# Moving the layer norms' combining of statistics from VectorE, tile by tile, to GpSimd, all tiles at once

## What is computed

```python
h = tok(x)                                        # frames @ DCT basis
h = h + attn(layernorm(h))
h = h + ffn(layernorm(h))

def attn(x):                                      # 4 heads
    n = layernorm(x, ln1_g, ln1_b)
    ...                                           # shift mix, q k v g, rmsnorm, decayed linear-attention scan
    x = x + (g * att) @ Wo.T
    return x + gelu(layernorm(x, ln2_g, ln2_b) @ W1.T) @ W2.T

def ffn(x):
    a = layernorm(x, ln_g, ln_b) @ attn_w.T + attn_b + x
    ...                                           # gelu(a @ fc1) @ fc2, gelu(. @ next_w)
```

## Time and profile before

| | us |
|---|---|
| median of 3 runs | 1221.79 |
| lowest, highest | 1215.12, 1226.37 |
| the profiled execution | 1218.9 |
| its span (first to last instruction) | 1217.1 |
| PE busy | 1138.9 (94%) |
| DVE busy | 986.5 (81%) |
| ACT busy | 621.5 (51%) |
| POOL busy | 300.9 (25%) |

### The profile page before, as it was taken

One profiled execution on the slowest core, in us unless ns is written; L12 is line 12 of the kernel. 1 busy time (PEld: TensorE's weight loads), 2 busy tenths in 40 slices (PEclk: granted clock), 3 DMA queues, 4 the chain that ended last, 5 costly groups with the idle time before them and its releaser, 6 DMA issues.

```text
span 1217.1 us, 43497 instructions
## 1 busy us (share of the span) xinstructions
PE 1138.9 (94%) x17955; PEld 807.8 (66%) x17955; DVE 986.5 (81%) x3362; ACT 621.5 (51%) x1100; POOL 300.9 (25%) x174
## 2 busy tenths in 40 slices
PE   4799999999999999999999999999999999999997
PEld 4576676666767676766666667666676766667664
DVE  7878788797887979788796887979879797987962
ACT  3346446363554736446363554736446364554634
POOL 4123131221403223131311403223131221403211
PEclk8799999999999999999999999999999999999999
DMA  5321313222141312313222141312313222141210
GB/s 188 106 64 39 113 43 110 65 79 56 43 132 44 87 47 66 110 43 113 63 78 55 44 130 46 88 45 63 112 44 110 63 80 57 43 132 45 87 55 17
DMA packets 51492, 91.48 MB, mean 75 GB/s; under 512 B 9536, under 2 KB 26592, under 8 KB 51296
## 3 DMA queue, kind: packets, MB, share of 16 engines
q1 hardware_dynamic: 51296, 88.69, 24.1%
HBM read 19.50 MB, written 9.78 MB: 24 GB/s over the span
## 4 chain that ended last, share of the span: by engine, by line
PE 83%; DVE 9%; POOL 4%; issue 3%; ACT 2%; DVEq 0%; POOLq 0%
PE bank L1056 10%; PE bank L1049 9%; PE bank L1084 9%; PE bank L1078 8%; PE bank L919 8%; PE bank L914 7%; PE bank L1014 7%; PE bank L998 5%; PE bank L990 4%; PE bank L1033 4%; POOL nrm L391 3%; PE bank L1029 3%; PE bank L954 3%; PE bank L943 2%; PE bank L994 2%
## 5 line engine op out<-in xcount | busy, mean ns | idle before, releaser
L514 ACT ACTIVATE px<-bank 128x512 f32<-128x512 f32 (+1 forms) x128 | 72.8, 569 | 218.0 <-PE bank L998 152.9
L763 DVE COPY_PREDICATED px<-mask,bank 128x512 f32<-128x512 uint32 (+1 forms) x128 | 88.6, 692 | 79.6 <-issue 76.8
L1078 PE MATMUL bank<-xa,f1w 128*128 128x512 f32 (+1 forms) x256 | 124.7, 587 | 14.8 <-DVE qtok L704 13.0
L1056 PE MATMUL bank<-w,hid 128*128 128x128 f32 x1024 | 121.9, 277 | 17.2 <-ACT hid L533 17.2
L1056 PEld LDWEIGHTS bank<-w,hid 128*128 128x128 f32 x1024 | 116.7, 192 | 31.6 <-ACT hid L533 31.6
L1014 PEld LDWEIGHTS bank<-qx,ki 128*32 128x32 f32 x7680 | 89.6, 110 | 42.3 <-issue 33.9
L827 DVE TENSOR_TENSOR ki<-k,rp 128x96 f32<-128x96 f32 (+13 forms) x512 | 113.2, 295 | 0.6 <-ACT k L499 0.6
L397 POOL TENSOR_TENSOR ab<-af,heads 128x896 f32<-128x896 f32 x16 | 40.8, 2552 | 291.1 <-DVE af L755 291.1
L1049 PE MATMUL bank<-c,w 128*128 128x512 f32 (+1 forms) x256 | 111.4, 568 | 1.1 <-ACT c L527 0.9
L1084 PE MATMUL bank<-hid,f2w 128*128 128x512 f32 (+1 forms) x256 | 107.5, 563 | 0.0
L1014 PE MATMUL bank<-qx,ki 128*32 128x16 f32 x7680 | 99.2, 193 | 6.9 <-issue 6.6
(11 more groups left out here) (142 smaller groups left out, 2414.0 us busy)
## 6 DMA issues: line engine op xcount, KB each, us to landing
qx<-qq SPq DMA_DIRECT2D x256, 96.0 KB
hs<-hs SPq DMA_DIRECT2D x32, 532.0 KB, 4.4
v<-v_f SPq DMA_DIRECT2D x16, 512.0 KB, 3.9
gz<-gate_f SPq DMA_DIRECT2D x16, 512.0 KB, 4.7
xT<-in_xT SPq DMA_DIRECT2D x16, 468.5 KB, 4.0
f1w<-in_fc1T SPq DMA_DIRECT2D x16, 256.0 KB, 2.7
f2w<-g_dram SPq DMA_DIRECT2D x16, 256.0 KB, 3.0
out<-t_sum SPq DMA_DIRECT2D x16, 256.0 KB, 2.7
```

Source lines behind the costliest of these rows:

```text
L763: V.copy_predicated(px[c % 2][0:n, :, 0:n], mask[0:n, 0:n].rearrange("p (o m) -> p o m", o=1).to_broadcast([n, HEADS, n]), bank[DIAG][0:n, ...
L1056: last = mm(dst[:, P * i:P * i + P], hid[:, j, P * m:P * m + P], w2[:, j, :], start=(j == 0), stop=(j == 3))
L1078: mm(dst[:, 0:width[g]], f1w[:, P * j:P * j + P], xa[:, cols(g)], start=True, stop=True).then_inc(f1_ok, 1)
```

## The change

The three pairs of DVE steps `gathered` and `vv` go. In their place GpSimd, ahead of each power, combines the even and odd numbers itself, for all tiles of the set at once: sum of the means and of the squared deviations, difference of the means, its square times 32, the sum of these, half the sum of means as the mean, and `vv` from the sum. Each instruction that reads what GpSimd has just written waits on GpSimd's own semaphore first. The order of the other work is kept, but GpSimd's first wait is now for `bn_stats` and not for `vv`.

```diff
+            def moments(st, mv, sums, odd, s, up, n):
+
+                gp.tensor_tensor(sums[:, s, :], st[:, s, 1:3], st[:, s, 4:6], ALU.add)
+                gp.tensor_tensor(odd[:, s], st[:, s, 1], st[:, s, 4], ALU.subtract).then_inc(up, 1)
+                gp.wait_ge(up, n + 1)
+                gp.tensor_tensor(odd[:, s], odd[:, s], odd[:, s], ALU.mult)
+                gp.tensor_scalar(mv[:, s, 0], sums[:, s, 0], 0.5, None, ALU.mult).then_inc(up, 1)
+                gp.wait_ge(up, n + 2)
+                gp.tensor_scalar(odd[:, s], odd[:, s], 32.0, None, ALU.mult).then_inc(up, 1)
+                gp.wait_ge(up, n + 3)
+                gp.tensor_tensor(odd[:, s], odd[:, s], sums[:, s, 1], ALU.add).then_inc(up, 1)
+                gp.wait_ge(up, n + 4)
+
+            def twice_normed(vv, odd, s, up, n):
+
+                gp.tensor_scalar(vv[:, s, 0], odd[:, s], 1.0 / P, EPS, ALU.mult, ALU.add)
+                gp.tensor_scalar(vv[:, s, 1], odd[:, s], (1.0 + EPS) / P, EPS * EPS, ALU.mult, ALU.add).then_inc(up, 1)
+                gp.wait_ge(up, n)
...
             def pow3(b, g):
-                gp.wait_ge(var3, nth(b, 2, g + 1))
+                gp.wait_ge(bn3, nth(b, 2, g + 1))
+                before(gp, n2_ok, b, 2, g + 1)
+                moments(st3, mv3, sm3, od3, four(g), mo3, nth(b, 10, 5 * g))
+                twice_normed(vv3, od3, four(g), mo3, nth(b, 10, 5 * g + 5))
...
-            def gathered(mv, st, ms, ag, count):
-                V.memset(tick[:, :], 0.0)
-                for m in ms:
-                    last = V.bn_aggr(mv[:, m, :], st[:, m, :])
-                last.then_inc(ag, 1)
-                dve.wait_ge(ag, count)
...
             def stats3(b, g):
                 dve.wait_ge(h1_ok, nth(b, 2, g + 1))
+                before(dve, r3_ok, b, 2, g + 1)
                 stats(h1, st3, bn3, g)
-                dve.wait_ge(bn3, nth(b, 2, g + 1))
-                gathered(mv3, st3, tiles(g), ag3, nth(b, 2, g + 1))
-                twice_normed(vv3, mv3, four(g)).then_inc(var3, 1)
```

More of the change, by code:

```diff
@@ L112, in program @@
         st1, vv1 = sb("st1", TILES, 6), sb("vv1", TILES, 2)
+        (sm1, od1), (sm2, od2), (sm3, od3) = ((sb(f"sm{i}", TILES, 2), sb(f"od{i}", TILES)) for i in (1, 2, 3))
         hl = sb("hl", PADT + 1)
@@ L169, in program @@
         ge2 = sem("ge2"); fin_ok = sem("fin_ok")
[L171 removed]
+        bn1 = sem("bn1"); mo1, mo2, mo3 = sem("mo1"), sem("mo2"), sem("mo3"); nl_ok = sem("nl_ok"); d_ok = sem("d_ok")
         mix = [sem(f"mix{i}") for i in range(4)]
@@ L376, in _ @@
             gp.memset(zq[:, :], 1.0)
+            gp.memset(hs0[:, SH:], 0.0)
             for tile in (hl, mixed[0], mixed[1]):
@@ L382, in _ @@
             gp.wait_ge(s_init, 2)
-            def pow1(b):
-                gp.wait_ge(var1, nth(b, 1, 1))
+            def moments(st, mv, sums, odd, s, up, n):
[13 more added lines that the diff above has]
+                gp.wait_ge(up, n)
+            def pow1(b):
+                all_ = slice(0, TILES)
+                gp.wait_ge(bn1, nth(b, 2, 2))
+                before(gp, hs1_in, b, 16, 16)
+                moments(st1, mv1, sm1, od1, all_, mo1, nth(b, 5, 0))
+                twice_normed(vv1, od1, all_, mo1, nth(b, 5, 5))
                 gp.tensor_tensor(rr1[:, :, :], vv1[:, :, :], nhalf[:, :].rearrange("p (m o) -> p m o", o=2), ALU.pow).then_inc(r1_ok, 1)
@@ L401, in pow2 @@
             def pow2(b, g):
-                gp.wait_ge(var2, nth(b, 2, g + 1))
+                gp.wait_ge(bn2, nth(b, 2, g + 1))
+                before(gp, nl2_ok, b, 2, g + 1)
+                moments(st2, mv2, sm2, od2, four(g), mo2, nth(b, 10, 5 * g))
+                gp.tensor_scalar(vv2[:, four(g)], od2[:, four(g)], 1.0 / P, EPS, ALU.mult, ALU.add).then_inc(mo2, 1)
+                gp.wait_ge(mo2, nth(b, 10, 5 * g + 5))
                 gp.tensor_tensor(rr2[:, four(g)], vv2[:, four(g)], nhalf[:, 0:4], ALU.pow).then_inc(r2_ok, 1)
@@ L642, in stats @@
                 last.then_inc(bn, 1)
-            def gathered(mv, st, ms, ag, count):
-                V.memset(tick[:, :], 0.0)
-                for m in ms:
-                    last = V.bn_aggr(mv[:, m, :], st[:, m, :])
-                last.then_inc(ag, 1)
-                dve.wait_ge(ag, count)
-            def twice_normed(vv, mv, s):
-                V.tensor_scalar(vv[:, s, 0], mv[:, s, 1], EPS, None, ALU.add)
-                return V.tensor_scalar(vv[:, s, 1], mv[:, s, 1], 1.0 + EPS, EPS * EPS, ALU.mult, ALU.add)
             def stats1(b, g):
                 dve.wait_ge(h_cp, nth(b, 2, g + 1))
+                before(dve, r1_ok, b, 1, 1)
                 stats(h, st1, bn1, g)
[L660 to L664, removed]
             def normed(b):
@@ L778, in stats2 @@
                 dve.wait_ge(x2_ok, nth(b, 2, g + 1))
+                before(dve, r2_ok, b, 2, g + 1)
                 stats(x2, st2, bn2, g)
-                dve.wait_ge(bn2, nth(b, 2, g + 1))
-                gathered(mv2, st2, tiles(g), ag2, nth(b, 2, g + 1))
-                V.tensor_scalar(vv2[:, four(g)], mv2[:, four(g), 1], EPS, None, ALU.add).then_inc(var2, 1)
             def normed2(b, g):
@@ L841, in body @@
                 if (b := at(1)) is not None:
[L842 to L846, removed]
+                    gated(b, 1); attended(b, 1); stats2(b, 1)
                 if (b := at(0)) is not None:
```

4 lines of the change are left out of this document (2 added, 2 removed).

## The result

| us | before | changed kernel |
|---|---|---|
| median of the runs taken side by side | 1219.97 (4 runs) | 1274.73 (4 runs) |
| lowest, highest | 1215.12, 1226.37 | 1269.59, 1275.95 |
| span of the profiled execution | 1217.1 | 1274.0 |
| PE busy, idle within the span | 1138.9, 78.2 | 1154.7, 119.3 |

The ratio is 1.0438, with a 95% interval of 1.0379 to 1.0496: 4.4% slower, 55 us. The sign was forecast, the size was not: 18.7 us were forecast, and the top of the range, 1259, is exceeded.

The account below looks back on a forecast made before the run. PE was taken as the bound, 94% busy, waiting 0.87 us a round for DVE's `qtok`. 15 x 1.2 + 0.7 = 18.7 us on the profiled 1218.9 gave 1237.6, stated as 1238, range 1221 to 1259.

Parts of the forecast that it names:

- The durations of small instructions: New GpSimd instructions: 0.20 us each, 0.10 more for a second in a group, 0.08 per wait; sets of 1.70 or 1.60 us.
- pow1 and pow2(1): First norm's set and half 1 of the second's: normed2(1) ends at 601.7, PE wants it at 602.01; no cost.
- a sign of being wrong: Prediction called itself wrong if, among other signs, PE's transposes of nl2(1) waited for DVE.
- dear instructions: Rival: 0.40 us per small instruction, PE waits 2.2 us at the transposes, 4.2 a round, 1282 us; chance 0.12.
- the term that counts: Third norm, half 0: DVE's `d` and mix hold GpSimd, `nb` 1.2 us too late each round, PE's `qtok` wait 2.1 us.
- the weaker: PE needs ACT's L538 after `nb` of normed3(0) only at 611.68, so `nb` may end at 609.98, against 609.41 via `qtok`.
- I price it at nothing: Third norm, half 1: DVE slips 0.8 us, but PE uses the spread q only at 630.82; no cost.
- The start: Bare chain at the kernel's start: 1.70 us in place of some 0.9 for eight tiles, +0.7 us.
- Too cheap: Rival: small instructions at 0.10 us cost 0.4 us a round, 1225; not held by DVE at all, 1219; chance 0.32.
- faster: Rival: powq(0) starts earlier and PE's 0.87 us wait a round shrinks, at most 13 us, 1206; chance 0.04.
- the tiles of normed hold GpSimd: Rival: pow2(1)'s groups wait for DVE's L672 tiles, PE waits 0.3 to 1.0 us more, up to 1253; chance 0.08.

Follow-up runs that it names:

- s12: Kernel before with the first norm's set and both halves of the second norm's combined on GpSimd, the third norm's on DVE; 1236.03 us, ratio 1.0121.
- free: Kernel before with only the first norm's set and half 0 of the second norm's combined on GpSimd; 1219.63 us, ratio 1.0025.
- s3: Kernel before with only the third norm's sets, both halves, combined on GpSimd; 1251.76 us, ratio 1.0249.
- s31: Kernel before with only half 1 of the third norm's statistics combined on GpSimd; 1241.18 us, ratio 1.0182.
- s30: Kernel before with only half 0 of the third norm's statistics combined on GpSimd; 1246.73 us, ratio 1.0220.
- afterlate: Changed kernel, all five sets on GpSimd, with normed3(1) moved behind the q levels on DVE; 1253.97 us, ratio to the kernel before 1.0306.
- x31late: s31 with normed3(1) moved behind the q levels on DVE; 1222.29 us, ratio to the kernel before 1.0029.
- swapb: Kernel before, no set on GpSimd, with x_attn(0) moved ahead of mixes(2) on DVE; 1205.09 us, ratio 0.9863.

## Why the prediction was right and wrong

**The durations of small instructions: right for one, wrong for a step.** 0.20 us for one is what the rows of pow1 show (0.20 to 0.24). The first pair starts 0.17 us apart, but from then on each instruction of pow1 starts 0.27 to 0.33 us after the one before, whether it waits for it or not: the second and third pair, taken as 0.10 more for their second instruction, cost a whole 0.27 more (622.74 to 623.01, 623.94 to 624.21). 2.22 us and 2.17 stand where 1.70 and 1.60 were forecast.

**pow1 and pow2(1), "no cost, but only 0.3 us of cover": the step that failed first.** The two sets are 1.09 us longer than forecast together, a cover of 0.3 was left, and PE waits 0.8 us a round at the transposes of nl2(1), which the prediction had named as a sign of being wrong. The working was right in its frame (the rival "dear instructions" named this very place, deciding "from 0.22 us an instruction on"), but I weighed the rival by the instruction's own duration, when what decides is the pitch, from start to start: 15 x 0.8 = 12 us of waits, +15.8 in all (s12). free shows that nothing is lost until pow2(1)'s set comes behind pow1's.

**pow3(0), "the term that counts": the mechanism right, the limit wrong.** Held by `d` and the mix as told: 4.0 us from first instruction to power (3.5 forecast), `nb` beside resid(1) 1.22 us, 2.69 us idle before it (2.4 forecast). But PE's wait at `qtok` did not grow from 0.87 to 2 us, it stayed 0.87. PE stops earlier, at the transposes behind ACT's L570, which I had called "the weaker" limit; and since the products of q's second half stand behind those, the loop from the transposes over ACT's squares, DVE's sums and powq back to PE is only shifted: from the transposes of `x` to the products it is 649.49 - 642.67 = 6.82 us, 6.68 before. The cost is 0.75 us a round at this place, 0.44 of it (6.6 us in s3) from pow3(0) and the rest with the first two norms' lateness. 10.5 us by s3 less s31, where 18 were forecast; alone it costs 27.1 (s30), where the 0.55 us that the forecast counts on are not there. One reading in the working is off: resid(1) ended 607.99 - 606.86 = 1.13 us after the mix's end, not 1.28; nothing in the sum rests on it.

**pow3(1), "I price it at nothing": wrong, and the largest.** Forecast 0.8 us of slip, "were no slack there, 0.8 us a round". It slipped 1.17 us, since this chain too is longer than forecast (2.14 us in place of 1.70), and its lateness cost 21.0 us alone and 18 to 21 in the changed kernel (afterlate), 1.2 to 1.4 us a round. I had looked for the first product that reads the spread q, saw 7 us up to it in a timeline of one round and took them for slack. But the q levels and the transfer lie in between. The records of the DMA packets show how much was left (us; half 0 of q is four DMAs of 32 packets):

```
kernel   first packet  last packet  PE's first product  PE's wait before it
before   626.98        629.47       630.82              0
x31late  628.49        630.99       632.33              0
changed  659.27        661.77       662.15              0.14
changed  279.69        283.39       283.92              1.48
```

In the kernel before PE begins 1.1 to 1.4 us after the last packet in every round but the first (0.75). In the changed kernel and in s31 it begins 0.38 to 0.59 us after it in nearly every round (0.74 once; in both the first round stands apart), and waits there. So of the 1.35 us some 0.96 were cover (an estimate: 1.35 less the shortest 0.39 or so). By it the forecast's own slip of 0.8 would have stayed inside, and 1.17 did not. What was late is the input of these products, and the profile names no engine for it.

**Where those 21 us are.** In s31 PE's idle time and busy time grew by 12.4 and 8.3 us. The idle part is the issue waits. From the restart of PE at L1078's place to the first product on the spread q it is 12.46 us in the mean before and 12.88 in s31, which is the late q: 0.4 us a round, 6 in all. From there to the next restart it is 60.49 and 61.37: 0.9 a round, 13 in all, lost behind the late q. In most rounds of the changed kernel the wait for q is short, as at 662.15. Its three longest (1.38, 1.48 and 0.97 us; the 1.48 is that at 283.92) fall where the spread's packets took 3.1 to 3.7 us in place of 2.5, with a piece of PE's code beside them.

These pieces bear on the rest as well. They come over the queue named instruction, 144 of 16 KB in the kernel before, the changed one and s31 alike, while DVE's and GpSimd's instructions change in number. ACT's 1100 are too few for 2.36 MB; for PE's 17955 products and as many weight loads it is 66 bytes each, so I take them for PE's code. In the profile of the changed kernel every stall of 0.35 us or more inside a run of L997 or L1021 ends 1.3 to 1.6 us after such a piece has arrived, as the records of that queue show (us):

```
kernel   piece starts, takes   arrives   stall ends, length
changed  663.14  1.55          664.69    666.06  0.75
changed  669.92  1.38          671.30    672.69  1.53
changed  740.09  1.75          741.84    743.30  0.94
changed  818.80  1.47          820.27    821.71  0.66
before   133.89  0.93          134.82    136.33  0.91
before   280.15  1.70          281.85    283.16  1.14
```

Of all 23 issue waits of the kernel before, 22 end 1.2 to 1.7 us after a piece arrived, of the changed kernel's 40 it is 32 (27.8 of 29.9 us), while such stretches cover only 7% of the span; the 8 others all stand before the first product on the spread q. Pieces took 0.9 to 1.5 us with no other packet beside them and up to 1.9 with many. A piece starts when PE has come to a point: for three in four of the 144, PE had by then begun the same number of instructions as before, to within 20. Products on the spread q are among the shortest of all (0.20 us each), so the code is used up fastest there; at 663.14 a piece starts one microsecond after PE began them, while the spread of q's other packets is still under way. That this is why more is lost behind the late q than the q is late by is what the records suggest; no run changed the fetch itself, so it stays argued. That the order on DVE decides it is shown (x31late).

**The busy time.** The granted clock is part of it. In the stretch from 700 to 800 us of the changed kernel (us, PE, PEld, DVE, ACT, POOL busy, PEclk, DMA share, GB/s)

```profile
700.00:800.00 100.00, 92.16 (x1244) 66.67 (x1243) 71.59 (x209) 48.37 (x87) 40.22 (x72) 0.97 0.22 67
```

and in that of the kernel before

```profile
700.00:800.00 100.00, 95.55 (x1759) 66.40 (x1758) 83.32 (x280) 54.47 (x99) 20.71 (x11) 1.00 0.30 88
```

the clock is 0.97 in place of 1.00: it stood at half (1.2 in place of 2.4 GHz) for 6.8 us from 745 us on, after the stall that ended at 743. After 75 us the clock was at half for 17.1 us in the changed kernel, in four pieces, 13.7 in s31, 3.4 in s12 and none in before. At half speed 17.1 us lose at most 8.6, of the 15.8 by which PE's busy time grew. x31late had 10.2 us of it and lost next to nothing, so the clock isn't what tells s31 from x31late. The remaining 7 us or more of busy time are not settled.

**The sum as it came out.** Priced places, in us: first and second norm 15.8 (forecast 0, or 0.7 with the start), third norm half 0 10.5 (18.0), half 1 21.0 (0): 47.3, and 7.5 more when all five sets are together. The start was forecast at +0.7 and came to 1.8 by the waits for `nl` of normed (4.6 us, 2.8 before). The two terms that the forecast set at nothing are 36.8 us, two thirds of the loss. The share of the third norm's halves hangs on which is counted first (27.1 and 4.4 by s30), but putting half 1's lateness right in the changed kernel gave back 18 to 21 us. And the forecast was 1237.6 for an execution 2.9 us below the median, so 1240.5 and not 1238 for the median.

**The rivals.** "Too cheap" is out by the held 1.15 us; "faster" is out, as the argument had it for this change, though its mechanism, powq(0) earlier and PE's 13 us gone, is real and was had in swapb by another edit. "Dear instructions" was the nearest to the truth in place and had a chance of only 0.12. Of "the tiles of normed hold GpSimd" there is a little: two of the tensor_scalar ones in pow2(1), beside L687's tiles, take 0.34 and 0.36 us, those of pow1 0.20 to 0.24. The Trainium skill (SBUF — State Buffer, section "Who interferes with whom") has two-input DVE instructions and GpSimd's excluding each other for their whole length; by the 1.15 us under `d` and the 1.14 under the mix the trace agrees. The other way round it does not in the kernel before, where `d` started beside a power and took its usual 1.14 us.

## What to carry to other kernels

On an engine that hands on by semaphore price a chain of small instructions by its pitch from start to start, not by the duration of one: here 0.27 to 0.33 us for 0.20. This error of 0.4 to 0.6 us a set stands behind both terms that were set at nothing. Before work moves onto the chain of a less busy engine, compare the length added with the cover at each consumer in turn, the last one in the round too, and where a transfer lies in between, count the slack from its last packet on; what DVE has queued behind a late instruction (here the q levels, for the sake of a norm that nobody is waiting for) is what it costs. The cure was then an order move: put the instruction that will be late behind work that others wait for. And where a wide two-input DVE instruction lies over a power on GpSimd that others wait for, move it: that alone gave 1.4%.

## What the runs showed of the hardware that was not expected

- A GpSimd instruction of 4 to 16 elements takes 0.20 to 0.24 us whatever its elements, if no DVE instruction holds it up; the first pair starts 0.17 us apart, and each later one 0.27 to 0.33 after the one before, with a wait or without. Beside DVE's tiles of normed it was up to 0.36 us and the pitch up to 0.45.
- Under a wide DVE instruction with two inputs in SBUF, a 0.2 us GpSimd instruction takes until its end: 1.15 and 1.14 us. A pair of wide ones holds two, since one step gets its turn between them.
- PE stands still for 0.2 to 1.8 us while nothing that the profile shows is missing, in 22 of 23 cases before and 32 of 40 in the changed kernel ending 1.2 to 1.7 us after a piece of code arrived. All such waits were 15.0 us of the kernel before, and 27.6 with normed3(1) 1.17 us late on DVE (s31).
- A wait for a DMA whose landing the profile does not show looks the same: PE began 0.38 to 0.59 us after the last packet of the spread q in nearly every round of the changed kernel, where it had begun 1.1 to 1.4 us after it before.
- Where a piece of code came beside it, the spread of half 0 of q took 3.1 to 3.7 us in place of 2.5 (three rounds of the changed kernel).
